# A two-layer graph network: GpSimd's work in a new order, the mask on ScalarE, and ScalarE's copy of the transposed attention ahead of a rectifier

## The reference

```
h = relu(layernorm(x));  x = x + L0(h, adj)     # attention, 8 heads of 64
h = relu(layernorm(x));  x = x + L1(h, adj)     # two hypergraph convolutions, 512 -> 1024 -> 512

L0:  feats = h W;  e = leaky_relu(e_self + e_neigh, 0.2) + (-1e10) * (1 - adj)
     out = relu(softmax(e) feats + b)
L1:  r = relu(G h W1 + b1);  r = layer_norm(r) * gamma + beta;  y = G r W2 + b2;  out = y + h
     G = D^-1 H B^-1 H^T,  H = (adj != 0)
```

## Time and profile before

| | |
|---|---|
| median of 3 runs | 2604.34 us (2603.8 to 2619.33) |
| the profiled execution, its own time | 2597.54 us |
| its span | 2595.7 us |
| mean granted TensorE clock, of full speed | 0.988 |
| turns | 128 |

### The profile page before, as it was taken

How to read it: one execution, slowest core, us unless ns; L and a number is a source line. 1 busy time by engine, 2 the same in 40 slices (tenths; PEclk the granted TensorE clock), 3 DMA queues, 4 the chain that set the end, 5 groups by cost and what they waited for, 6 DMA issues and landing times. The chain is left out here.

```text
span 2595.7 us, 50200 instructions
## 1 busy us (share of the span) xinstructions
PE 2453.2 (95%) x13972; PEld 2104.9 (81%) x13972; DVE 2042.6 (79%) x4256; ACT 1638.9 (63%) x4233; POOL 1758.6 (68%) x1940
## 2 busy tenths in 40 slices
PE   3799999999999999999999999999999999999997
PEld 2588888888888888888888888888888888888886
DVE  4778788788788788788788788788788788788784
ACT  2466666666666666666666666666666666666663
POOL 4566677676676676676677677677677676676662
PEclk8799999999999999999999999999999999999998
DMA  5244444444544444544444444444444444544532
GB/s 189 78 120 132 136 127 136 135 127 136 137 127 131 136 127 131 137 128 125 128 132 128 139 128 129 137 129 132 137 128 137 134 128 133 137 126 133 137 107 69
DMA packets 656394, 336.16 MB, mean 130 GB/s; under 512 B 554608, under 2 KB 570992, under 8 KB 656368
## 3 DMA queue, kind: packets, MB, share of 16 engines
q1 hardware_dynamic: 638512, 303.35, 41.9%
q10 hardware_dynamic: 17856, 32.51, 3.6%
HBM read 234.50 MB, written 101.26 MB: 129 GB/s over the span
## 5 line engine op out<-in xcount | busy, mean ns | idle before, releaser
L474 ACT ACTIVATE att<-u,shifts 128x128 f32<-128x128 f32 x1024 | 404.8, 395 | 91.2 <-DVE shifts L775 87.7
L877 PE MATMUL p_w1a<-W_hi,rT_hi 128*128 128x512 f32 x1024 | 418.9, 409 | 1.6 <-ACT rT_hi L582 1.6
L878 PE MATMUL p_w1a<-W_lo,rT_hi 128*128 128x512 f32 x1024 | 408.2, 399 | 0.0
L475 ACT ACTIVATE att_low<-u,shifts 128x128 f32<-128x128 f32 x1024 | 402.3, 393 | 0.0
L396 POOL TENSOR_TENSOR u<-u,mask 128x1024 f32<-128x1024 f32 x128 | 306.9, 2398 | 89.8 <-DMA u<-en_rows 88.8
L951 PE MATMUL p_att<-feats,attT 128*128 128x65 f32 x2048 | 259.2, 280 | 71.5 <-ACT attT L509 71.5
L951 PEld LDWEIGHTS p_att<-feats,attT 128*128 128x128 f32 x2048 | 241.5, 194 | 97.0 <-ACT attT L509 97.0
L409 POOL TENSOR_TENSOR rs<-ve,halfpow 128x1 f32<-128x1 f32 x128 | 70.9, 554 | 365.3 <-DVE ve L811 365.3
L649 DVE TENSOR_TENSOR att<-att,att_low 128x512 f32<-128x512 f32 x256 | 218.3, 853 | 98.4 <-POOL rs L409 94.6
L372 POOL TENSOR_TENSOR xc<-xT_in,u 128x512 f32<-128x512 f32 x128 | 281.7, 2201 | 11.5 <-DMA u<-en_rows 11.5
L502 ACT ACTIVATE raw<-raw 128x512 f32<-128x512 f32 x128 | 81.3, 635 | 312.9 <-DVE raw L741 312.9
(11 more groups left out here) (124 smaller groups left out, 7167.4 us busy)
## 6 DMA issues: line engine op xcount, KB each, us to landing
u<-en_rows SPq DMA_DIRECT2D x130, 576.0 KB, 3.7
r_blocks<-raw SPq DMA_DIRECT2D x128, 512.0 KB, 2.6
raw<-r_blocks SPq DMA_DIRECT2D x512, 128.0 KB, 3.7
xT_in<-in_xT SPq DMA_DIRECT2D x128, 256.0 KB, 3.1
out<-raw SPq DMA_DIRECT2D x128, 256.0 KB, 2.0
x_in<-in_x ACTq DMA_DIRECT2D x124, 256.0 KB, 3.2
adj_in<-in_adj SPq DMA_DIRECT2D x128, 128.0 KB, 2.4
en_rows<-eT SPq DMA_DIRECT2D x520, 1.1 KB
```

What stands on the lines that cost most here:

```text
L474: nc.scalar.activation(att[:, i, :], u[:, g.slot(2), i, :], ACT.Exp, bias=shifts[:, 0, i:i + 1])
L475: last = nc.scalar.activation(att_low[:, i, :], u[:, g.slot(2), i, :], ACT.Exp, bias=shifts[:, 1, i:i + 1], scale=SLOPE)
L877: mm(dst, hi, w_hi, start=first, stop=False)
L878: mm(dst, hi, w_lo, start=False, stop=False)
```

## The change

ScalarE copies p_att to attT before it rectifies r's second half, and rectifies the centred x before r's first half. The mask is one ScalarE activation, adj * 2^36 - 2^36, in place of two GpSimd operations. GpSimd's turn begins with the addition to u, then xc (for t+4 in this turn instead of t+3 in the next), rs2, the two additions for `rest` (of graph t instead of t+1), rs1 and nb, beT, G_lo and z_lo, and rs0 (for t+5 instead of t+4). The tile o_sc lies in PSUM instead of SBUF. VectorE's last L649 of a turn waits for nb instead of rs1. The diff without its repeated lines:

```diff
-        o_sc = raw[:, 1, 2 * D:3 * D]
...
+        o_sc = p_ta[:, :]
...
             def turn(t):
-                g = t.plus(3)
-                if g.within(NG):
-
-                    pool.wait_ge(s_xT[g.slot(2)], g.uses(2, 16))
-                    pool.wait_ge(s_en_bc, g.count(per=16))
...
-                    nc.gpsimd.tensor_tensor(mask[:, :], ones[:, :], adj_in[:, g.slot(4), 0, :], ALU.subtract).then_inc(s_absent, 1)
-                    pool.wait_ge(s_absent, g.count())
-                    nc.gpsimd.tensor_tensor(mask[:, :], mask[:, :], absent[:, :].broadcast_to([P, N]), ALU.mult).then_inc(s_mask, 1)
...
+                g = t.plus(4)
+                if g.within(NG):
+
+                    pool.wait_ge(s_xT[g.slot(2)], g.uses(2, 16))
+                    pool.wait_ge(s_en_bc, g.count(per=16))
+                    if g.has(1):
+                        pool.wait_ge(s_h0_lo, g.count(1))
+                    nc.gpsimd.tensor_tensor(xc[:, :, :], xT_in[:, g.slot(2), :, :],
...
-                g = t.plus(1)
-                if g.within(NG):
 
                     s, s4 = g.slot(2), g.slot(4)
-                    if g.has(4):
-                        pool.wait_ge(s_y_sb, g.count(4))
                     pool.wait_ge(s_h, g.count())
                     pool.wait_ge(s_x1, g.count())
                     nc.gpsimd.tensor_tensor(rest[s4], x1[:, s, :], h[:, s, :], ALU.add).then_inc(s_xh, 1)
...
+                g = t.plus(5)
+                if g.within(NG):
...
                     rstd(g, mv0, ve0, rs0[:, g.slot(4):g.slot(4) + 1], s_mv0, s_ve0, s_rs0)
...
-                    act.wait_ge(s_pre, g.count(per=2))
-                    nc.scalar.activation(r[:, HALF:DH], r[:, HALF:DH], ACT.Relu, accum_out=sum2[:, 1:2]).then_inc(s_r, 1)
+                g = t.plus(2)
+                if g.within(NG):
+
+                    act.wait_ge(s_in[g.slot(4)], g.uses(4, 32))
+                    if g.has(1):
+                        act.wait_ge(s_u, g.count(1))
+                    nc.scalar.activation(mask[:, :], adj_in[:, g.slot(4), 0, :], ACT.Identity, bias=absent[:, :],
+                                         scale=-ABSENT).then_inc(s_mask, 1)
...
                     nc.scalar.activation(attT[:, :, :].rearrange("p h n -> p (h n)"), p_att[:, :],
                                          ACT.Copy).then_inc(s_attT_sb, 1)
+                g = t
+                if g.within(NG):
+                    act.wait_ge(s_pre, g.count(per=2))
+                    nc.scalar.activation(r[:, HALF:DH], r[:, HALF:DH], ACT.Relu, accum_out=sum2[:, 1:2]).then_inc(s_r, 1)
...
-                        dve.wait_ge(s_rs1, t.plus(1).count())
+                        dve.wait_ge(s_nb1, t.plus(1).count())
                     larger(t.plus(2), 0)
```

More of the change, by code:

```diff
@@ L179, in gnn_two_layers @@
         s_e_blk, s_es_low, s_eT, s_en_out, s_en_bc, s_u = (sem("s_" + n) for n in ("e_blk", "es_low", "eT", "en_out", "en_bc", "u"))
-        s_absent, s_mask, s_max, s_neg_s, s_neg_m, s_shifts, s_att = (sem("s_" + n) for n in ("absent", "mask", "max", "neg_s", "neg_m", "shifts", "att"))
+        s_mask, s_max, s_neg_s, s_neg_m, s_shifts, s_att = (sem("s_" + n) for n in ("mask", "max", "neg_s", "neg_m", "shifts", "att"))
         s_exp, s_attT, s_attT_sb, s_o, s_rden, s_osc, s_x1 = (sem("s_" + n) for n in ("exp", "attT", "attT_sb", "o", "rden", "osc", "x1"))
@@ L364, in turn @@
             def turn(t):
-                g = t.plus(3)
+                g = t.plus(2)
+                if g.within(NG):
+                    pool.wait_ge(s_mask, g.count())
+                    pool.wait_ge(s_en_bc, g.plus(2).count(per=16))
+                    nc.gpsimd.tensor_tensor(u[:, g.slot(2), 0:HEADS, :], u[:, g.slot(2), 0:HEADS, :],
+                                            mask[:, :].unsqueeze(1).broadcast_to([P, HEADS, N]), ALU.add).then_inc(s_u, 1)
+                g = t.plus(4)
                 if g.within(NG):
@@ L372, in turn @@
                     nc.gpsimd.tensor_tensor(xc[:, :, :], xT_in[:, g.slot(2), :, :],
-                                            u[:, g.plus(2).slot(2), HEADS, :].unsqueeze(1).broadcast_to([P, DC, N]),
+                                            u[:, g.slot(2), HEADS, :].unsqueeze(1).broadcast_to([P, DC, N]),
                                             ALU.subtract).then_inc(s_xc, 1)
-                g = t.plus(2)
-                if g.within(NG):
-                    pool.wait_ge(s_in[g.slot(4)], g.uses(4, 32))
-                    if g.has(1):
-                        pool.wait_ge(s_u, g.count(1))
-                    nc.gpsimd.tensor_tensor(mask[:, :], ones[:, :], adj_in[:, g.slot(4), 0, :], ALU.subtract).then_inc(s_absent, 1)
-                    pool.wait_ge(s_absent, g.count())
-                    nc.gpsimd.tensor_tensor(mask[:, :], mask[:, :], absent[:, :].broadcast_to([P, N]), ALU.mult).then_inc(s_mask, 1)
-                g = t.plus(4)
-                if g.within(NG):
-                    if g.has(1):
-                        pool.wait_ge(s_rs0, g.count(1))
-                    if g.has(4):
[L389 to L397, removed]
                 g = t
@@ L403, in turn @@
                     nc.gpsimd.tensor_tensor(rs2[:, g.slot(2):g.slot(2) + 1], ve2[:, :], halfpow[:, :], ALU.pow).then_inc(s_rs2, 1)
+                    s, s4 = g.slot(2), g.slot(4)
+                    pool.wait_ge(s_h, g.count())
+                    pool.wait_ge(s_x1, g.count())
+                    nc.gpsimd.tensor_tensor(rest[s4], x1[:, s, :], h[:, s, :], ALU.add).then_inc(s_xh, 1)
+                    if g.base == 0:
+                        pool.wait_ge(s_small, SMALL * 16)
+                    pool.wait_ge(s_xh, g.count())
+                    nc.gpsimd.tensor_tensor(rest[s4], rest[s4], b2_bc[:, :], ALU.add).then_inc(s_rest, 1)
                 g = t.plus(1)
@@ L419, in turn @@
                     nc.gpsimd.tensor_copy(beT[:, N:N + 1], adj_in[:, g.slot(4), 1, 0:1]).then_inc(s_row, 1)
-                g = t.plus(1)
-                if g.within(NG):
-                    s, s4 = g.slot(2), g.slot(4)
-                    if g.has(4):
-                        pool.wait_ge(s_y_sb, g.count(4))
[L426 to L432, removed]
                 g = t.plus(-1)
@@ L442, in turn @@
                     nc.gpsimd.tensor_tensor(z_lo[:, :], z[:, :], z_hi[:, :], ALU.subtract).then_inc(s_z_lo, 1)
+                g = t.plus(5)
+                if g.within(NG):
+                    if g.has(1):
+                        pool.wait_ge(s_rs0, g.count(1))
+                    if g.has(4):
+                        pool.wait_ge(s_feats_sb, g.count(4, per=2))
+                        pool.wait_ge(s_es_low, g.count(4))
+                    rstd(g, mv0, ve0, rs0[:, g.slot(4):g.slot(4) + 1], s_mv0, s_ve0, s_rs0)
             turns(pool, turn, NG, {-3: setup_w0, 0: setup_w2})
@@ L482, in turn @@
                     exps(t.plus(1), 1)
[L483 to L487, removed]
                 g = t.plus(3)
@@ L496, in turn @@
                 if g.within(NG):
+                    act.wait_ge(s_pre, g.count(per=2) - 1)
+                    nc.scalar.activation(r[:, 0:HALF], r[:, 0:HALF], ACT.Relu, accum_out=sum2[:, 0:1]).then_inc(s_r, 1)
+                g = t
+                if g.within(NG):
                     act.wait_ge(s_r, g.count(per=2) - 1)
@@ L756, in turn @@
                         dve.wait_ge(s_rB_out, g.count(1, per=16))
+                    if g.base == 0:
+                        dve.wait_ge(k_lo2, 2)
                     nc.vector.transpose(rB, r[:, :]).then_inc(s_rB, 1)
```

## The result

| | before | changed |
|---|---|---|
| median of the runs | 2607.05 us (2603.8 to 2619.33) | 2697.23 us (2696.08 to 2699.5) |
| the profiled execution, its own time | 2597.54 us | 2697.33 us |
| its span | 2595.7 us | 2695.5 us |
| a steady turn, by the starts of L931 (median) | 19.35 us | 20.32 us |

The changed kernel takes 1.0359 times as long as the one before (95% interval 1.0311 to 1.0407).

What follows compares the result with a forecast made beforehand. TensorE's own work plus its wait for ScalarE's copy was taken as the bound; 125 x 0.89 = 111 us on 2597.5 gave 2708.5, plus 6.8 to the runs' median: 2715 us, range 2570 to 2870.

Steps and rivals of the forecast that it cites:

- The wait at L951 goes: TensorE's second attention product no longer waits for ScalarE's copy, worth 71.5 to 97.0 us if nothing else were late.
- The second chain starts 0.70 later: The chain from r's second-half rectifier through VectorE's transpose (L757) to h: L757 at 2.83 instead of 2.13.
- L768 at 5.29, L770 at 5.49: VectorE operations after the maximum, in us from the attention transposes' start; perhaps 0.1 quicker without the wait for u.
- nb alone, 0.53 less: GpSimd's nb no longer runs beside VectorE's L649, making the chain to h 0.53 us shorter.
- o_sc in PSUM, 0.06 more: VectorE's L792, reading o_sc from PSUM, takes 0.06 us more; the write by L784 was taken as nothing.
- L428 at 5.35, between L768 and L770: GpSimd's first addition to rest starts right behind rs2, 5.35 us into the turn, between two VectorE operations.
- L770 held, L775 at 6.71, h at 10.88, L981 at 11.74: GpSimd's first addition to rest holds VectorE's tiny L770; L775 comes at 6.71 instead of 5.00, delaying h and TensorE's G product.
- A turn 0.89 longer, 125 times: Each of some 125 steady turns 0.89 us longer than 19.36, 111 us in all.
- Rival 1: Both GpSimd additions to rest hold VectorE: a turn 2.07 us longer, 2863 us; chance 20%.
- Rival 2: GpSimd's first addition shifts behind L775 in part of the turns; at half of them 2655 to 2660 us; chance 10%.
- Rival 3: GpSimd's first addition doesn't hold VectorE's small operations: a turn of 19.24 us, 2577 to 2589 us; chance 15%.
- Rival 4: TensorE never waits at L981 and the whole wait at L951 is gained: 2507 to 2533 us; chance 10%.

Runs made afterwards that it cites:

- e4_only_copy: The kernel before with one edit, ScalarE's copy to attT ahead of the rectifier of r's second half: 2626.85 us, 1.0148 of the kernel before.
- e8_rs1: The changed kernel with VectorE's last L649 of a turn waiting for rs1 again, not nb: 2797.65 us, 1.0751 of the kernel before.
- e7_o_sc_sbuf: The changed kernel with o_sc in SBUF as before: 2715.4 us, 1.0434 of the kernel before, 0.75% above the changed kernel.
- e1_rest_late: The changed kernel with GpSimd's two additions for rest moved from behind rs2 to behind beT: 2556.85 us, 0.9871 of the kernel before.
- e6_pieces: The changed kernel with GpSimd's first addition for rest cut in four pieces of 128 columns: 2614.47 us, 1.0045 of the kernel before.
- e2_relu_first: The changed kernel with the rectifier of r's second half ahead of the copy again: 2592.37 us, 0.9989 of the kernel before.
- both moves: The changed kernel with the additions for rest behind beT and the rectifier of r's second half ahead of the copy: 2496.03 us, 0.9640 of the kernel before.
- the two single edits: The edits of e1_rest_late and e2_relu_first, each alone in the changed kernel: 0.9871 and 0.9989 of the kernel before.

## Why the prediction was right

The forecast was 2715 us, in a range of 2570 to 2870; measured are 2697. By the steps of the prediction:

- **The wait at L951 goes.** Right: the copy at 1.08, L951 at 2.34, no wait.
- **The second chain starts 0.70 later.** Right: L757 at 2.83 as forecast; e4_only_copy has this step alone, and its turn is 0.38 longer.
- **L768 at 5.29, L770 at 5.49.** They are at 5.21 and 5.41, the 0.1 that I had left open because the maximum no longer waits for u. It changed nothing, since L770 ends when the addition does.
- **nb alone, 0.53 less.** Right: nb takes 0.19, and e8_rs1 gives the 0.53 back in the median turn.
- **o_sc in PSUM, 0.06 more.** Wrong in size: L792 takes 0.69 from PSUM as it did from SBUF, L784 0.70 where it took 0.69. I took the price from L828, which also multiplies by a factor for each partition, where L792 has a constant; which of the two differences makes L828 0.06 longer no run separates. What the place in PSUM gives is the 0.13 a turn of e7_o_sc_sbuf, which I had not priced.
- **xc 1.26 where VectorE doesn't hold it.** Right: 1.29, and GpSimd was free before ve2 came.
- **L428 at 5.35, between L768 and L770.** Right within 0.01 (5.36). The sum of four handovers from four rows held. It did not have to be so exact: in the ten turns where the addition missed L770 it held L775, at nearly the same length of turn.
- **L770 held, L775 at 6.71, h at 10.88, L981 at 11.74.** They came at 6.72, 10.84 and 11.70. e1_rest_late shows the cause by taking it away, e6_pieces by changing the length of the instruction that holds.
- **A turn 0.89 longer, 125 times.** 0.97 by the medians, since the next L931 came 8.63 after L981 instead of 8.51: L981 takes 1.16 after a wait and 1.05 without. That is some 10 us more than the 111 of the sum. Against it, the long single turns of the kernel before (one of 25.0 at 1225 us) fell away, some 13 us by the mean turn of 19.46 against the median of 19.35, and the first turns were 8.5 faster: the sum of 111 stands beside 99.8 of the spans and 90 of the medians. That these errors go against each other, and leave the forecast 18 us off, is luck; the collision and its size are not.

Rival 1, both additions holding VectorE, came true in no turn. L775 started 0.01 to 0.09 ahead of the second addition in the 115 turns with L770 held, 0.02 in most, and was never held. Even so the lead of 0.02 us that I argued with was a weak reason: in e2_relu_first VectorE had as much against the first addition and lost three turns in four. What decides such a race was not settled. Rival 2, L392 behind L775 in a part of the turns, came true in one turn of the middle (19.46 long). Rival 3, no collision, is e1_rest_late: 19.21 a turn against the 19.24 worked out. Rival 4, TensorE as the bound, needed both moves: 18.64 a turn.

The rule of the Trainium skill, page "SBUF — State Buffer", section "SBUF: two separate sides", that of a VectorE operation with two SBUF inputs and a GpSimd operation that reads SBUF whichever starts first has the shared ports for its whole instruction, is borne out for a scalar_tensor_tensor on 128x8 from SBUF (1.27 us in place of 0.17) and for the 128x512 one, which is free once one input lies in PSUM. It is not seen for rs2, which held L768 in none of 126 turns, and in e2_relu_first VectorE, whose recorded start was the earlier one by 0.01 to 0.04 in 92 turns, waited in 66 of them. The 115 ns of that page's section "A bandwidth-pool intuition that's wrong (but worth ruling out)" are from the end of a VectorE operation until a DMA whose descriptors GpSimd writes is served, which no run here shows; L770, VectorE behind GpSimd, ended 0.02 us after the addition.

## What to carry to other kernels

A wait of the bounding engine is worth what the next chain leaves of it: before an edit moves one instruction past another, ask who waits for the one that is moved back. Here the wait at L951 was 0.6 a turn, and the chain behind the displaced rectifier had 0.35 to spare.

Where VectorE and GpSimd work in the same memory, place GpSimd's long operations away from VectorE's chain of short ones, or cut them in pieces: an operation of 8 elements a partition waits for a whole 1.3 us addition. And judge an edit against the kernel that it was made in. Against the kernel before, the two single edits look worth little (1.3% faster, and nothing) and both together 3.6%; against the changed kernel's turn they take off 1.11 and 0.58 us alone and 1.68 together, so their gains simply add up.

## What the runs showed of the hardware that was not expected

- In e8_rs1 TensorE waited 1.98 us in every turn and got the lower clock (1.2 GHz) for a stretch of 3.4 us in every fifth or sixth (23 such stretches between 200 us and the last L931, none or one in each of the other nine traces). With a wait of 1.45 or 1.6 a turn (the changed kernel, e7_o_sc_sbuf) it kept 2.4 GHz from 210 us to the last turns. The low stretches cost 35 us, half of what the longer wait cost itself.
- Moving o_sc to PSUM cost its two 128x512 VectorE operations next to nothing: L792 took 692 ns with it in PSUM and in the kernel before with it in SBUF, L784 700 ns into PSUM and 692 into SBUF.
- What a GpSimd instruction does to VectorE's short operations depends on which it is: the 1.3 us addition on 128x512 holds L770, rs2 on 128x1, 0.55 us long, holds L768 in none of 126 turns. Why was not tested.
- Where two starts lie within 0.04 us of each other, a turn is 18.7 or 19.8 long by who gets through first (e2_relu_first). A kernel with such a race has a spread of turns. By an estimate from these two lengths (1.04 us of 19.7), an edit elsewhere that shifts one side a little may show as a gain or loss of some per cent that is not its own; no run tried it.
